# One whole model program on one core: GpSimd's sends spread out one by one, VectorE making the last product of each group, and the second expert layer's weights loaded one by one

## What is computed

```python
x = x + linear_attention(layernorm(x))  # 16 heads of 64, relu features phi, out / (phi_q . sum phi_k)
x = x + experts(layernorm(x))           # softmax over 8 experts, best 2 renormalized, F = 512
x = x + fast_weight_memory(layernorm(x))
x = x + experts(layernorm(x))           # the same weights' shapes, again routed

def linear_attention(h):                # b, n, 128
    q, k, v = heads(h @ W_qkv)
    phi_q, phi_k = relu(q @ RF), relu(k @ RF)
    out = phi_q @ (phi_k.T @ v) / (phi_q @ phi_k.sum(n) + 1e-6)
    return out @ W_out + b_out

def experts(h):
    g = softmax(h @ Wr); w, id = top_k(g, 2); w = w / w.sum()
    return sum(w[i] * (relu(h @ W1[id[i]]) @ W2[id[i]]) for i in 0, 1)

def fast_weight_memory(h):              # 8 steps in sequence for each of 512 columns and 16 heads
    q, k, v, beta = heads(h @ w_qkvb.T)
    q, k = normalized(elu(q) + 1), normalized(elu(k) + 1)
    for t in steps: W = W + beta[t] * (v[t] - W @ k[t]) * k[t].T;  out[t] = W @ q[t]
    return layer_norm(h + (scaled out) @ w_o.T, ln_g, ln_b)
```

## Time and profile before

| | |
|---|---|
| median of three runs | 1131.63 us (1125.02 to 1134.97) |
| profiled execution, its own time | 1121.75 us |
| its span | 1120.0 us, 31388 instructions |
| mean granted clock of PE | 0.933 |
| busy shares | PE 86%, PEld 65%, DVE 48%, ACT 48%, POOL 34% |
| costliest group | PE L1717, 256 matmuls, 120.7 us busy |
| second expert layer | 893 to 1088 us |

### The profile page before, as it was taken

One profiled execution on the slowest core, in us unless ns is written; L12 is line 12 of the kernel. 1 busy time (PEld: TensorE's weight loads), 2 busy tenths in 40 slices (PEclk: granted clock), 3 DMA queues, 4 the chain that ended last, 5 costly groups with the idle time before them and its releaser, 6 DMA issues.

```text
span 1120.0 us, 31388 instructions
## 1 busy us (share of the span) xinstructions
PE 967.3 (86%) x11919; PEld 724.6 (65%) x11919; DVE 539.4 (48%) x1908; ACT 541.3 (48%) x1082; POOL 378.5 (34%) x391
## 2 busy tenths in 40 slices
PE   7999999999897699969987998898889887557990
PEld 6455666656697699945445745754576787557990
DVE  4246535544562322155695687368767564130103
ACT  2444343343043355537666666646646454225770
POOL 2201233222245565530412012331332254455551
PEclk9999999999897899989999999989989898788995
DMA  8633432134031232050202100201071211112316
GB/s 219 177 78 78 94 96 65 43 90 91 25 80 51 75 83 64 29 151 4 77 3 76 42 21 23 92 15 50 21 229 46 52 52 42 48 51 74 86 35 227
DMA packets 83506, 82.75 MB, mean 74 GB/s; under 512 B 12335, under 2 KB 64388, under 8 KB 82848
## 3 DMA queue, kind: packets, MB, share of 16 engines
q1 hardware_dynamic: 68864, 58.30, 20.0%
q0 software_dynamic: 10176, 19.04, 5.4%
q10 hardware_dynamic: 4320, 3.41, 1.1%
HBM read 53.96 MB, written 27.64 MB: 73 GB/s over the span
## 4 chain that ended last, share of the span: by engine, by line
PE 32%; DVE 8%; issue 6%; ACT 5%; another core or an unknown queue 2%; POOL 1%; DMA 1%; SPq 0%; ACTq 0%; POOLq 0%; DVEq 0%
PE b_ring L1717 6%; PE b_ring L1282 6%; PE b_ring L1271 5%; PE b_g L1761 4%; PE b_g L1736 3%; PE b_ring L1684 2%; ACT early L1881 2%; PE b_ring L1776 2%; DVE b_kq L2114 2%; DMA early<-expert_parts 1%; ACT b_outT L1893 1%; POOL b_last_pair L1573 1%; DVE b_outT L110 1%; DVE b_prod L2030 1%
## 5 line engine op out<-in xcount | busy, mean ns | idle before, releaser
L1717 PE MATMUL b_ring<-b_hT,b_qkT 128*128 128x512 f32 x256 | 120.7, 609 | 6.0 <-DVE b_kq L2114 5.9
L1282 PE MATMUL b_ring<-wide,b_v 128*128 x568 | 81.3, 289 | 26.8 <-issue 16.1
L2114 DVE SCALAR_TENSOR_TENSOR b_kq<-b_exp,b_ring 128x512 f32<-128x512 f32 x128 | 83.1, 683 | 39.8 <-ACT b_exp L1867 38.5
L1271 PE MATMUL b_ring<-b_v,b_kq 128*128 128x128 f32 x568 | 81.2, 289 | 16.5 <-issue 11.1
L276 POOL DMA_INDIRECT expert_rows<-f_route_sent,f_route_place_id x64 | 62.0, 969 | 94.9 <-DVE f_route_place_id L232 50.9
L1282 PEld LDWEIGHTS b_ring<-wide,b_v 128*128 128x128 f32 x568 | 74.2, 204 | 28.3 <-issue 28.1
L1271 PE MATMUL a_ring<-phik 128*128 128x128 f32 x568 | 78.7, 284 | 12.9 <-ACT phik L1292 11.9
L1867 ACT ACTIVATE b_exp<-b_ring 128x512 f32<-128x512 f32 x128 | 73.5, 604 | 31.9 <-PE b_ring L1717 20.1
L1271 PEld LDWEIGHTS b_ring<-b_v,b_kq 128*128 128x128 f32 x568 | 74.4, 204 | 18.9 <-issue 12.5
L1717 PEld LDWEIGHTS b_ring<-b_hT,b_qkT 128*128 128x128 f32 x256 | 45.2, 189 | 62.2 <-issue 37.6
L1282 PE MATMUL a_wide<-wide,phiqT 128*128 x568 | 78.4, 283 | 5.6 <-ACT phiqT L1297 3.5
(11 more groups left out here) (331 smaller groups left out, 1906.4 us busy)
## 6 DMA issues: line engine op xcount, KB each, us to landing
a_rn_wide<-norm_compact SPq DMA_DIRECT2D x28, 512.0 KB, 10.1
wide<-in_L_ffn_W SPq DMA_DIRECT2D x32, 256.0 KB, 6.1
a_rn_wide<-expert_rows SPq DMA_DIRECT2D x71, 65.0 KB
b_coef<-gram_compact SPq DMA_DIRECT2D x4, 1024.0 KB, 4.9
early<-expert_parts SPq DMA_DIRECT2D x16, 256.0 KB, 5.1
b_hT<-expert_rows SPq DMA_DIRECT2D x56, 65.0 KB
x<-in_L_attn_a_x SPq DMA_DIRECT2D x8, 256.0 KB, 4.3
early<-expert_parts SPq DMA_DIRECT2D x4, 512.0 KB, 5.9
```

The lines of the kernel that those rows point to most:

```text
L1271: ins = pe.matmul(self.hid_bank[j % 2][:, f * P:(f + 1) * P], self.w1_now[:, b % W1_SLOTS, f * P:(f + 1) * P], self.blkT[:, b % HID_SLOTS, ...
L1282: ins = pe.matmul(self.y_bank[j % 2][:, 0:P], self.hidT[:, b % HID_SLOTS, f, :], self.C["w2"][:, bass.ds(e, 1), f, :].rearrange("p a c -> ...
L1717: pe.matmul(ring[n % 4][:, :], w, hT[:, g % 2, half * 512:half * 512 + 512], start=True, stop=True)\
L2114: dve.scalar_tensor_tensor(out=kq[:, p % 2, half:half + FOURS // 2, slot:slot + T * FOUR], in0=exps[:, n % EXPS, :].rearrange("p (a n) -> ...
```

## The change

- Every send but the first of a route now has a wait or another instruction ahead of it (route 4: `hid_done` of the expert blocks; routes 5 to 7 of the second layer and 6 and 7 of the first: one send behind each scatter).
- In the fast weight memory the sends of routes 0, 2 and 3 wait for points of the mixing (mixed_full) and of the values (v_full); those of route 1 alternate with `pair_last` and with kq_full. Roots and `ln_out.root` (small POOL instructions) move with them.
- DVE makes the product of each group's last head pair (`end_pair`, semaphore pair_ended) in place of POOL's `pair_last(g, 7)`; it stands behind the group's last kq and ahead of `build(g - 1, 0)`.
- SP loads the sixteen pieces of weights one by one, behind waits for mixed_full and v_full; `store_mix(3)` and `load_mix(3)` stand behind the sixth.
- Two of the solution's parts move from ahead of keys_and_queries(3) to its n = 12 and 13; five of those beside keys_and_queries(1) move one n later; `add_parts(1)` and `statistics(1)` go to n = 11 and 19 of group 0; `residual(3)` stands ahead of `route_statistics(5)`.

```diff
@@ linear attention, POOL
+        def pace_last(i):
+            if i == 1:
+                return kv_done, 3 * LAST + 3
+            if i == 3:
+                return norm_done, LAST + 1
+            if i in (5, 7):
+                return spread_done, (i - 3) // 2
+            return y_done, NT * (LAST - 1) + i // 2 + 1
...
-                    if i and t < LAST:
-                        sem, count = pace(t, i)
+                    if i:
+                        sem, count = pace(t, i) if t < LAST else pace_last(i)
                         wait_apart(pool, sem, count, K.passed)
                     router.send_one(pool, t - 2, i)
@@ first expert layer, POOL
-                elif j == 10:
-                    route_slot(LAST - 1)
-                    router.send(pool, LAST - 1)
-                elif j == 16:
-                    route_slot(LAST)
-                    router.send(pool, LAST)
+                for r, first in ((LAST - 1, 10), (LAST, 18)):
+                    if first <= j < first + 2 * NT:
+                        route_slot(r)
+                        router.send_one(pool, r, j - first)
@@ fast weight memory, SP
-            load_experts(sp, C, inp, C["w_in"][1])
-            store_mix(NG - 1)
-            load_mix(NG - 1)
+            for e in range(EXPERTS):
+                for k in range(2):
+                    if e == 3 and k == 0:
+                        store_mix(NG - 1)
+                        load_mix(NG - 1)
+                    i = 2 * e + k
+                    sem, count = (S["mixed_full"], 32 + 7 + 2 * i) if i < 5 else (S["v_full"], 48 + 2) if i < 6 \
+                        else (S["mixed_full"], 48 + 1 + i - 6)
+                    wait_apart(sp, sem, count, K.passed)
+                    load_expert(sp, C, inp, C["w_in"][1], e, k)
@@ fast weight memory, POOL
-            send(0)
-            ln_out.root(pool, C["minus_half"], 1)
+            for i in range(2 * NT):
+                sem, count = (S["mixed_full"], 16 + 10 + 2 * i) if i < 3 else (S["v_full"], 32 + 1 + 3 * (i - 3))
+                wait_apart(pool, sem, count, K.passed)
+                router.send_one(pool, route(0), i)
+                if i == 4:
+                    ln_out.root(pool, C["minus_half"], 1)
             shift(3)
-            for i in range(2 * NT):
-                router.send_one(pool, route(1), i)
-                if i >= 4 and i % 2 == 0:
-                    pair_last(3, i // 2 - 2)
-            pair_lasts(3, 2, 5)
+            for p in range(NT):
+                pair_last(3, p)
+                router.send_one(pool, route(1), 2 * p)
+                wait_apart(pool, S["kq_full"], 32 * 3 + 4 * p + 7, K.passed)
+                router.send_one(pool, route(1), 2 * p + 1)
+            pair_last(3, 4)
...
-            send(2)
+            for i in range(2 * NT):
+                sem, count = (S["mixed_full"], 32 + 12 + 2 * i) if i < 2 else (S["v_full"], 48 + 1 + 5 * (i - 2) // 2)
+                wait_apart(pool, sem, count, K.passed)
+                router.send_one(pool, route(2), i)
             ln_out.root(pool, C["minus_half"], 2)
             for i in range(2 * NT):
                 if i == NT:
                     root(4)
+                wait_apart(pool, S["mixed_full"], 48 + 3 + i, K.passed)
                 router.send_one(pool, route(3), i)
@@ second expert layer, POOL
             for i in range(2 * NT):
-                if i == NT:
+                if i == 2:
                     root(5)
+                elif i == 4:
                     ln_out.root(pool, C["minus_half"], 3)
+                if i:
+                    wait_apart(pool, ffn.F["hid_done"], ffn.first + i, K.passed)
                 router.send_one(pool, route(4), i)
-            for j in range(BLOCKS):
+                if i >= 3:
+                    ffn.scatter(pool, i - 3)
+            for j in range(2 * NT - 3, BLOCKS):
                 ffn.scatter(pool, j)
-                if j == 1:
+                if j == 6:
                     root(6)
-                elif j == 3:
-                    for i in range(2 * NT):
-                        if i == NT:
-                            root(7)
-                        router.send_one(pool, route(5), i)
-                elif j == 8:
-                    send(6)
-                elif j == 15:
-                    send(7)
+                elif j == 11:
+                    root(7)
+                for r, first in ((5, 7), (6, 16), (7, 24)):
+                    if first <= j < first + 2 * NT:
+                        router.send_one(pool, route(r), j - first)
@@ fast weight memory, PE
                 def products(p):
-                    pe.wait_ge(S["last_paired"], PAIRS * g + p + 2)
+                    if p < PAIRS - 1:
+                        pe.wait_ge(S["last_paired"], (PAIRS - 1) * g + p + 2)
+                    else:
+                        pe.wait_ge(S["pair_ended"], g + 1)
@@ fast weight memory, DVE
-            BEFORE = {1: 1, 2: 11, 3: 9}
-            BESIDE = {1: (2, 4, 6, 8, 10, 11, 12, 13, 14, 15, 16, 17, 18, 19, 20), 2: (1, 4, 6, 8, 10),
-                      3: (1, 3, 4, 6, 8, 9, 10)}
+            BEFORE = {1: 1, 2: 11, 3: 7}
+            BESIDE = {1: (3, 5, 7, 9, 10, 11, 12, 13, 14, 15, 16, 17, 18, 19, 20), 2: (1, 4, 6, 8, 10),
+                      3: (1, 3, 4, 6, 8, 9, 10, 12, 13)}
...
+            def end_pair(g):
+                key, query = KEYS + (T - 1) * FOUR, QUERIES + (T - 1) * FOUR
+                dve.tensor_tensor(last_pair[:, 1, :].rearrange("p (a b) -> p a b", b=FOUR),
+                                  kq[:, 1, :, key:key + FOUR], kq[:, 1, :, query:query + FOUR], ALU.mult)\
+                    .then_inc(S["pair_ended"], 1)
...
+                dve.wait_ge(S["kq_ready"], g * 32 + 32)
+                end_pair(g)
                 if g > 0:
                     build(g - 1, 0)
...
+            residual(3)
             route_statistics(5)
-            residual(3)
```

26 lines of the change are left out of this document (15 added, 11 removed).

## The result

The changed kernel took 1084.69 us in the median of four runs (1081.61 to 1087.63), the kernel before 1128.83 us in its four; the ratio is 0.9604, with a 95% interval of 0.9547 to 0.9661. The forecast was 1079.5 us. The profiled execution took 1081.61 us beside a span of 1079.9 us, at a granted clock of 0.960 where it was 0.933.

A forecast was written before the change was run, and what follows sets the result against it. It held that PE gets instructions at a trickle while POOL issues indirect DMAs without pause. Terms of 26.1 plus 6 and 20 us took 1121.75 to 1069.6; plus 9.9 gave 1079.5 us, range 1046 to 1115.

The forecast's parts named there:

- the likeliest case: Whole kernel: interleaved expert blocks take 3.0 to 3.4 us each, giving 1079.5 us, or 1066 to 1091; chance 0.50.
- Last body: Linear attention's last body: paced sends end the gulps of 64 matmuls and slow L879; gain 8.5 us (6 to 9).
- Mixing 1: Fewer sends beside mixing 1 cut the wait of ACT's copies from 9.51 us; gain 6.2 us, 3 to 8.
- Mixing 2: PE gets 8.8 us back at mixing 2, but build(3, 0) waits behind it; gain 3.5 us (0 to 8).
- Mixing 3: Its eight sends go two per head pair, beside ACT's copies of build; gain 3.5 us (0 to 6).
- VectorE's last product and the two steps: Group ends: product gains 0.5 us in each of three groups; two solution steps leave the stretch before DVE's first keys, 1.5.
- First expert layer: One send behind each of scatters 10 to 25, blocks at 3.2 us; gain 6 us (16 to -3).
- Second expert layer: Blocks 0 to 31: 28 at 3.2 us and six at 1.90, 101 us for 121.2; gain 20 (38 to 3).
- E: Rival: the holes don't come from the sends' density; only 4.4 us of gains are left, 1127 us; chance 0.08.
- C: Rival: POOL's pace alone sets the interleaved expert blocks, 2.55 us each; 1050 us; chance 0.14.
- D: Rival: two indirect DMAs per expert block keep POOL without a pause, slower beyond 4.4 us a block; 1165 at 5.2; chance 0.09.
- B: Rival: interleaved expert stretches run at the low clock, 3.8 us a block, gaining nothing there; 1105 us; chance 0.19.

The follow-up runs named there:

- e2: The kernel before with only the sends moved to their new places, none of the other edits: 1090.55 us, ratio 0.9667.
- e1: The changed kernel with every POOL send put back where it stood before, the other edits kept: 1125.51 us against 1130.02, ratio 0.9964.
- e11: The changed kernel with POOL making each group's last product again and statistics(1) back at n = 26: 1027.0 us, ratio 1.0056.
- e12: The changed kernel, memset of 384 floats behind expert-layer sends and scatters, awaited only ahead of the next memset, statistics(1) at n = 26: 1056.8 us, ratio 1.0359.
- e10: The changed kernel, memset of 192 floats behind each expert-layer send and scatter, awaited only ahead of the next memset: 1036.73 us, ratio 1.016.
- e3: Bench replacing the model: PE runs matmuls that wait for nothing while POOL issues DMAs or memsets; 28.85 us undisturbed, 52.7 beside 24 unpaused indirect DMAs.
- e4: The same bench with other stages: fewer rows, other memset pauses, short runs of DMAs; DMAs 1.53 to 1.64 us apart cost nothing.
- e9: The kernel before, memset of 192 floats behind each send from the last body on and each scatter: 1160.34 us, ratio 1.0299.

## Why the prediction was right, step by step

The time lay in the range and the sign was right, by the likeliest case. The steps, against the table:

- *Last body*: 8.5 forecast, 7.0 measured, or 6.3 in e2. The 1.7 us gained ahead of it are no send's doing, since e1 has them too. The pauses of L858 and the slow L879 went as described.
- *Mixing 1*: 6.2 forecast, 7.3. *Mixing 2*: 3.5 forecast, 8.7 - 5.3 = 3.4, for the reason given: build(3, 0) waits for the coefficients' DMA, and PE for it. *Mixing 3*: 3.5 forecast, 3.0.
- *VectorE's last product and the two steps*: 3.0 forecast for groups 1 to 3. PE's wait at its sum went from 2.40 to 0.18 us, and ACT's copy, named as next, took 1.60 us: 0.6 us less in the two waits together, and 0.5 in group 2 (2.31, then 0.12 and 1.66), as priced. But a stage doesn't get shorter by that alone: keys 1 gave 0, keys 2 0.6, keys 3 got 1.0 longer. The comparison with e2 (56.2 us) tells why: the paced sends themselves cost keys 3 4.8 us, which I had not forecast, and the product and the steps gave 3.9 of them back.
- *Group 0*: the moves of `add_parts(1)` and `statistics(1)` I didn't price. Keys 0 lost 0.5 us in the fourth and 1.0 us in the fifth eighth of its matmuls, and e2, without the moves, takes the 44.0 us of before. Yet the moves aren't shown to be the cause: the fifth eighth takes 6.2 us in the changed kernel, but 6.5 in e11 and e12, which have `statistics(1)` back at n = 26, and 5.2, as before, in e10, which has it at n = 19. This is open. Of e1's 2.6 us, 1.2 lie in the first eighth, at half the clock.
- *First expert layer*: 3.2 us a block forecast, 51.2 / 16 = 3.2 measured; blocks 10 to 26 gain 5.6 where 6 were forecast. The whole layer gains only 3.6, since the last sends now run two blocks further (+3.3 us in blocks 26 to 32).
- *Second expert layer*: 20, and 1.4 for the residual, forecast; 15.6 measured. The stretch that was priced came out: from the weighing of block 0 (873.76 us) to that of block 31 (975.78 us) it took 102.0 us, where 101 were forecast and 121.2 were needed before. It was not even, 3.4 us a block in blocks 10 to 26 (54.1 us). What was put at nothing without a reason is what comes behind: blocks 32 to 45 took 31.3 us, 24.7 before, where 1.90 each was assumed. The window's row shows the lost time and the low clock:

```profile
976.00:1008.00 32.00, 28.39 (x230) 28.20 (x229) 2.56 (x6) 18.25 (x49) 16.28 (x16) 0.89 0.33 86
```

These tails, 3.3 and 6.6 us, are most of what the two expert layers fell short by.
- *The weights*: 0 forecast; e1 shows that they did no harm and made no gain.

The sum of the profiled executions is 40.1 us, 12 less than the 52.1 of the forecast. That the median came within 5.2 us owes something to luck: I added the 9.9 us by which the kernel before's median stood above its profiled execution, and the changed kernel's stands only 3.1 above.

Of the rivals, E (the density of the sends has nothing to do with it) is refuted by e3, and by e1 beside e2; C (2.55 us a block) and D (over 4.4) by the block times; B needs a block of 3.8 us at half the clock, and the granted clock was 0.90 in blocks 10 to 26 of the first layer, 0.91 in those of the second and 0.92 over the whole second layer. E leaned on the Trainium skill, Runtime: NRT & Kernel Launch, section Instruction fetch mechanics: the sequencer streams its own code and the cost is mostly hidden. The bench's trace agrees with that, for no code was under way from 43 to 79 us, while PE stood. What E drew from it, that sends could then not starve PE, doesn't follow, and my own "gets its instructions at a trickle" names something that no run shows either.

Of the signs, these held: the 64 matmuls in 1.96 us, sends at most two in a row ahead of the expert layers, the gap at the last product ended by ACT. These did not: the second expert layer took 185.6 us and not 170 to 178, its longest hole was 6.40 us and not 4, and ACT waited 7.33 us at the mixing's copy (L1928, the old L1893), at the head of mixing 3 behind the late `build`. Of the signs of being wrong none appeared, D's narrowly: its holes were to be of 7 us or more.

What I had wrong in kind is something that no rival held: I took the starving for a property of the kernel, and it is one of the occasion on which it runs.

## What to carry to other kernels

When an engine waits for "issue" or an unshown releaser, look at what another engine issues at that moment; here the spacing of the DMAs of an engine that was busy 34% of the time was worth 39.5 us. Where GpSimd's indirect DMAs starve TensorE, it takes a stream of them to do it: in the bench, runs of four with a pause behind them cost nothing, nor did 26 us at 1.53 us from one to the next. Spread them, but not past the point at which somebody needs them. And run the kernel before beside every variant: this change is a ratio of 0.96 where TensorE starves, and where it doesn't, its nearest relative was 0.6% slower than the kernel before.

## What the runs showed of the hardware

- In a stream of 24 indirect DMAs of GpSimd, 1.16 to 1.29 us apart, each costs TensorE 1.0 to 1.1 us, whether it moves 128 rows of 520 bytes, 128 of 64 bytes or 32 rows of 520 (e3, e4). At 1.46 us apart it costs 0.51 us. At 1.53 us nothing is lost in the 26 us that the stage lasted. 24 direct DMAs 0.53 us apart cost nothing.
- TensorE's holes begin late, 10.6 us into a stream at 1.27 us and 18.6 us into one at 1.46 us, and end 3.9 us behind the stream's last DMA (e3). No packet of code is under way meanwhile.
- The effect came and went between occasions for the same kernel before: 1120.74 to 1134.98 us beside e1 to e9, 1017.66 to 1024.43 us beside e10 to e12. The number of the chip doesn't tell them apart. The cause is open; no run here could reach it.
- A pause on GpSimd costs more than its instruction: a memset of 0.29 us with a wait behind it added 0.94 us to a scatter (2.21 against 1.27), because the next DMA's preparation lost its cover; with the wait moved behind the next DMA it added 0.15 (1.42).
